# Split products instead of plain fp32 ones in the tail of a decoder layer, and its attention heads' outputs split in place

## The reference

```python
x = x + attn(layernorm(x))          # gated delta rule, 16 heads of 128, then @ Wout (2048 x 512)
x = x + xattn(layernorm(x), ctx)    # energy = (ctx Wq^T + bq)(ctx Wk^T + bk)^T; attention = softmax(energy)
                                    # x_m = layernorm(x) @ attention^T          ("attended")
x = x + ffn(layernorm(x))           # logits = xf Wg^T; gate = argmax of softmax, 8 experts of rank 64
                                    # h = xf A^T (8 x 64 = 512 columns), masked to the chosen expert  ("up")
                                    # y = h Bw^T * 4 * prob of the chosen expert                       ("down")
```

## Time and profile before

| | us |
|---|---|
| median of 3 runs | 2031.08 |
| lowest and highest | 2026.42, 2033.64 |
| profiled execution, span from its first to its last instruction (the only time the page has for it) | 2031.7 |
| its stretch from 1589 us to the end (the tail) | 443 |

### The profile page before, as it was taken

How to read it: one execution, slowest core, us unless ns; L and a number is a source line. 1 busy time by engine, 2 the same in 40 slices (tenths; PEclk the granted TensorE clock), 3 DMA queues, 4 the chain that set the end, 5 groups by cost and what they waited for, 6 DMA issues and landing times.

```text
span 2031.7 us, 45678 instructions
## 1 busy us (share of the span) xinstructions
PE 1915.2 (94%) x16962; PEld 1561.4 (77%) x16962; DVE 1128.8 (56%) x2048; ACT 934.1 (46%) x2987; POOL 743.1 (37%) x1143
## 2 busy tenths in 40 slices
PE   5899999999999999999999998999997799999999
PEld 3688888888888888888888887888886565656574
DVE  5656565665656575656656665657563442534433
ACT  2455554646464555646464645555563321213121
POOL 1255453636363554536363535445452000000000
PEclk9899998999998999989999999989997899999999
DMA  3011111112010111111120101021114513121110
GB/s 101 16 33 32 33 40 25 34 30 42 22 38 22 38 32 33 39 25 37 28 43 22 38 22 38 23 41 34 31 24 144 146 36 93 42 83 52 55 27 21
DMA packets 220196, 87.10 MB, mean 43 GB/s; under 512 B 138320, under 2 KB 204240, under 8 KB 219280
## 3 DMA queue, kind: packets, MB, share of 16 engines
q1 hardware_dynamic: 220048, 84.83, 16.4%
HBM read 57.28 MB, written 27.53 MB: 42 GB/s over the span
## 4 chain that ended last, share of the span: by engine, by line
PE 49%; issue 25%; POOL 10%; DVE 7%; ACT 4%; DMA 3%; SPq 1%; POOLq 1%; DVEq 0%; ACTq 0%
PE bank L558 17%; PE bank L858 4%; PE bank L808 3%; DVE vT L1406 2%; POOL blkT L1774 2%; PE bank L817 2%; PE bank L770 2%; POOL prod L1770 2%; PE bank L759 2%; PE bank L678 2%; ACT vv L1074 2%; PE bank L802 2%; POOL k_tok L1740 2%; PE bank L824 1%; DMA blkT_d<-blkT 1%
## 5 line engine op out<-in xcount | busy, mean ns | idle before, releaser
L558 PE MATMUL bank<-x_hi,w_hi 128*128 128x512 f32 x1024 | 433.5, 423 | 13.4 <-DVE vT L1406 7.1
L558 PE MATMUL bank<-x_hi,w_lo 128*128 128x512 f32 x1024 | 410.3, 401 | 0.0
L558 PE MATMUL bank<-x_lo,w_hi 128*128 128x512 f32 x1024 | 408.7, 399 | 1.1 <-issue 1.1
L558 PEld LDWEIGHTS bank<-x_hi,w_hi 128*128 128x128 f32 x1024 | 197.9, 193 | 56.1 <-issue 13.9
L558 PEld LDWEIGHTS bank<-x_hi,w_lo 128*128 128x128 f32 x1024 | 196.7, 192 | 43.8
L558 PEld LDWEIGHTS bank<-x_lo,w_hi 128*128 128x128 f32 x1024 | 197.7, 193 | 33.2 <-issue 1.6
L1406 DVE SCALAR_TENSOR_TENSOR qT<-bank,cw,qT 128x511 f32<-128x511 f32 (+2 forms) x192 | 142.1, 747 | 51.1 <-ACT qT L1041 46.5
L1830 POOL TENSOR_TENSOR rstd<-ve,mhalf 128x1 f32<-128x1 f32 x32 | 17.4, 544 | 386.8 <-DVE ve L1588 386.8
L1406 DVE SCALAR_TENSOR_TENSOR kT<-bank,cw,kT 128x511 f32<-128x511 f32 (+2 forms) x192 | 143.3, 747 | 9.9 <-ACT kT L1041 4.9
L1206 ACT ACTIVATE o_tmp<-bank 128x128 f32<-128x128 f32 x256 | 67.4, 278 | 175.5 <-PE bank L824 175.5
L1406 DVE SCALAR_TENSOR_TENSOR vT<-bank,cw,vT 128x511 f32<-128x511 f32 (+2 forms) x192 | 143.2, 746 | 6.8 <-ACT vT L1041 2.3
(11 more groups left out here) (221 smaller groups left out, 4446.2 us busy)
## 6 DMA issues: line engine op xcount, KB each, us to landing
w_raw<-in_w_heads SPq DMA_DIRECT2D x64, 256.0 KB, 2.8
o_d<-og SPq DMA_DIRECT2D x64, 256.0 KB, 2.6
o_raw<-o_d SPq DMA_DIRECT2D x16, 1024.0 KB, 6.2
x_in<-in_x SPq DMA_DIRECT2D x16, 256.0 KB, 3.3
blkN_d<-nT SPq DMA_DIRECT2D x64, 64.0 KB, 2.1
t<-blkT_d SPq DMA_DIRECT2D x64, 64.0 KB, 2.4
wo_raw<-in_w_out SPq DMA_DIRECT2D x4, 1024.0 KB, 9.1
x_res<-in_x SPq DMA_DIRECT2D x16, 256.0 KB, 2.7
```

The source lines that it names most:

```text
L558: last = mm(bank[bk][:, :], w[:, kind % 2, d, :], xx[:, d, b * S:(b + 1) * S], start=(n == 0), stop=(n == 3 * ND - 1))
```

## The change

- attended, up and down are each made of three float32r products of high and low parts, accumulated in the same bank: xlT_hi, xlT_lo with attT_hi, attT_lo; xfT_hi, xfT_lo with a_hi, a_lo; hmT_hi, hmT_lo with b_hi, b_lo. The logits stay plain fp32 on xfT. TensorE waits within a product for the low part.
- ScalarE's copies write the high parts (with xfT also the plain one); VectorE gets ln_low, att_low and hm_low, each a subtraction of the high part from the PSUM bank, 16 per batch. A transpose that takes a bank again waits for the low part too.
- a and b are split once, in batch 0: high parts on ScalarE, low parts on VectorE, in place of a_sb and b_sb.
- o_lo lies where o_raw lies, so load_heads waits for the output product two chunks before, not for its split.
- xlT is held for three chunks instead of four and xfT for two, so that ScalarE's copies of later chunks wait for products (xm_mm, h_mm). hm, hmT and y_out are placed elsewhere, the four heads_over semaphores become one.
- On VectorE the next batch's second o_split moves behind layernorm(1,0), and the low parts are put between the other steps; on ScalarE route(0) moves ahead of ln_copy(1,3).

```diff
@@ sync
-                        sp.wait_ge(olo_done, t - 1)
+                        sp.wait_ge(oproj_mm, t - 1)
@@ tiles
+    a_lo = at(place["a_sb"][0], "a_lo", [P, ND, E * R], F32R)
+    o_lo = at(place["o_raw"][0], "o_lo", [P, 2, H, P], F32R)
+    xlT_hi = tl("xlT_hi", [P, 3, ND, P], F32R)
+    xfT_hi = tl("xfT_hi", [P, 2, ND, P], F32R)
@@ tensor, ln_transpose
                     if n >= 2:
                         pe.wait_ge(lnT_done, 8 * b + n - 1)
+                        pe.wait_ge(lnT_low, 8 * b + n - 1)
@@ tensor, attended
-                        last = mm(bank[c % 2][:, :], xlT[:, c, k, :], attT[:, k, :], start=(k == 0), stop=(k == ND - 1))
+                        mm(bank[c % 2][:, :], xlT_hi[:, c % 3, k, :], attT_hi[:, k, :], start=(k == 0), stop=False)
+                    pe.wait_ge(lnT_low, 8 * b + c + 1)
+                    for k in range(ND):
+                        mm(bank[c % 2][:, :], xlT_lo[:, c % 3, k, :], attT_hi[:, k, :], start=False, stop=False)
+                    if c == 0:
+                        pe.wait_ge(attT_low, 4 * b + 4)
+                    for k in range(ND):
+                        last = mm(bank[c % 2][:, :], xlT_hi[:, c % 3, k, :], attT_lo[:, k, :], start=False, stop=(k == ND - 1))
@@ tensor, up
-                        last = mm(bank[c % 2][:, :], xfT[:, c, k, :], a_sb[:, k, :], start=(k == 0), stop=(k == ND - 1))
+                        mm(bank[c % 2][:, :], xfT_hi[:, c % 2, k, :], a_hi[:, k, :], start=(k == 0), stop=False)
+                        mm(bank[c % 2][:, :], xfT_hi[:, c % 2, k, :], a_lo[:, k, :], start=False, stop=False)
+                    pe.wait_ge(lnT_low, 8 * b + 4 + c + 1)
+                    for k in range(ND):
+                        last = mm(bank[c % 2][:, :], xfT_lo[:, c % 2, k, :], a_hi[:, k, :], start=False, stop=(k == ND - 1))
@@ scalar, ln_copy
+                    if stage == 0:
+                        if c == 3:
+                            act.wait_ge(xm_mm, 4 * b + 1)
+                        fn(xlT_hi[:, c % 3, :, :], grid(2 + c % 2), ACT.Copy).then_inc(lnT_done, 1)
+                    else:
+                        act.wait_ge(h_mm, 4 * b + max(c - 1, 0))
+                        fn(xfT[:, c % 2, :, :], grid(2 + c % 2), ACT.Copy)
+                        fn(xfT_hi[:, c % 2, :, :], grid(2 + c % 2), ACT.Copy).then_inc(lnT_done, 1)
@@ vector
+                def ln_low(stage, c):
+                    dve.wait_ge(lnT_done, 8 * b + 4 * stage + c + 1)
...
+                    tt(low, grid(2 + c % 2), high.bitcast(F32), ALU.subtract).then_inc(lnT_low, 1)
@@ vector, order in a batch
                 maximum(3)
+                ln_low(0, 0)
                 o_split(b, 3)
                 residual(0, 1)
                 attention(2)
                 attention(3)
                 layernorm(0, 1)
+                if first:
+                    for i, (low, raw, high) in enumerate(((a_lo, a_sb, a_hi), (b_lo, b_sb, b_hi))):
+                        dve.wait_ge(ab_hi_done, i + 1)
+                        tt(low[:, :, :], raw[:, :, :], high[:, :, :].bitcast(F32), ALU.subtract).then_inc(ab_lo_done, 1)
+                ln_low(0, 1)
+                att_low(0)
+                att_low(1)
                 residual(0, 2)
                 layernorm(0, 2)
                 if more:
                     o_split(b + 1, 0)
                 residual(0, 3)
+                att_low(2)
+                att_low(3)
                 layernorm(0, 3)
+                ln_low(0, 2)
+                ln_low(0, 3)
+                residual(1, 0)
+                layernorm(1, 0)
                 if more:
                     o_split(b + 1, 1)
-                for c in range(NC):
+                for c in (1, 2):
                     residual(1, c)
                     layernorm(1, c)
+                ln_low(1, 0)
+                residual(1, 3)
+                layernorm(1, 3)
+                ln_low(1, 1)
+                ln_low(1, 2)
...
                 route(0)
+                ln_low(1, 3)
                 route(1)
+                hm_low(0)
                 route(2)
+                hm_low(1)
                 result(0)
                 route(3)
+                hm_low(2)
                 result(1)
+                hm_low(3)
```

More of the change, by code:

```diff
@@ L204, in layer @@
     kx = tl("kx", [P, S])
-    attT = tl("attT", [P, NC, S])
+    hm = at(place["qx"][0], "hm", [P, 2, D])
+    attT_hi = tl("attT_hi", [P, NC, S], F32R)
+    attT_lo = tl("attT_lo", [P, NC, S], F32R)
     x_res = tl("x_res", [P, NC, D])
     xl = tl("xl", [P, 2, D])
[L208 to L212, removed]
+    xlT_hi = tl("xlT_hi", [P, 3, ND, P], F32R)
+    xlT_lo = tl("xlT_lo", [P, 3, ND, P], F32R)
+    xfT = tl("xfT", [P, 2, ND, P])
+    xfT_hi = tl("xfT_hi", [P, 2, ND, P], F32R)
+    xfT_lo = tl("xfT_lo", [P, 2, ND, P], F32R)
+    a_hi = tl("a_hi", [P, ND, E * R], F32R)
+    b_hi = tl("b_hi", [P, E * R // P, D], F32R)
     t_small = Plan(consts_end)
@@ L319, in layer @@
     y_store = [sem("y_store0"), sem("y_store1")]
-    heads_over = [sem(f"heads_over_{e}") for e in ("pe", "act", "dve", "pool")]
+    ab_hi_done, ab_lo_done, lnT_low, attT_low, hmT_low = (
+        sem(n) for n in ("ab_hi_done", "ab_lo_done", "lnT_low", "attT_low", "hmT_low"))
+    heads_over = sem("heads_over")
     held = sem("held")
@@ L477, in _ @@
             head(H - 1, False)
[L480 to L481 removed]
+            sp.wait_ge(heads_over, 4)
             for s in og_out:
@@ L938, in down @@
                     for k in range(E * R // P):
-                        last = mm(bank[4 + c % 2][:, :], hmT[:, c % 2, k, :], b_sb[:, k, :],
-                                  start=(k == 0), stop=(k == E * R // P - 1))
+                        mm(bank[4 + c % 2][:, :], hmT_hi[:, c % 2, k, :], b_hi[:, k, :], start=(k == 0), stop=False)
+                        mm(bank[4 + c % 2][:, :], hmT_hi[:, c % 2, k, :], b_lo[:, k, :], start=False, stop=False)
+                    pe.wait_ge(hmT_low, 4 * b + c + 1)
+                    for k in range(E * R // P):
+                        last = mm(bank[4 + c % 2][:, :], hmT_lo[:, c % 2, k, :], b_hi[:, k, :],
+                                  start=False, stop=(k == E * R // P - 1))
                     last.then_inc(y_mm, 1)
@@ L1241, in _, with batch @@
             o_split(0, 1)
-            def batch(b, more):
+            def batch(b, first, more):
                 def exponentials(m):
@@ L1271, in batch @@
                 o_split(b, 3)
+                if first:
+                    fn(a_hi[:, :, :], a_sb[:, :, :], ACT.Copy).then_inc(ab_hi_done, 1)
+                    fn(b_hi[:, :, :], b_sb[:, :, :], ACT.Copy).then_inc(ab_hi_done, 1)
                 ln_copy(0, 1)
@@ L1555, in o_split, with batch @@
                 tt(o_lo[:, c % 2, :, :], o_raw[:, c % 2, :, :], o_hi[:, c % 2, :, :].bitcast(F32), ALU.subtract).then_inc(olo_done, 1)
-            for s in heads_over:
-                dve.wait_ge(s, 1)
+            dve.wait_ge(heads_over, 4)
             o_split(0, 0)
             o_split(0, 1)
-            def batch(b, more):
+            def batch(b, first, more):
                 def maximum(m):
```

82 lines of the change are left out of this document (54 added, 28 removed).

## The result

The changed kernel takes 2021.12 us (median of 4 runs, 2017.27 to 2023.73) against 2032.36 us before (4 runs, 2026.42 to 2036.67): a ratio of 0.9945, 95% interval 0.992 to 0.997, so faster, by half a percent. The forecast was 2016.9 us, a ratio of 0.993. Counted from these medians the change took 11.2 us; the forecast had 14.2. Its profiled execution took 2023.73 us with a span of 2022.0, so 1.7 us lie around the span, which the page of before did not show.

A forecast was written before the change was run, and what follows sets the result against it. TensorE was taken to bound the tail, working 419.57 of 443 us. Batch gains of 0.55, 4.75, 4.75 and 4.1 summed to 14.2 us, from the 2031.08 median to 2016.9 us; range 2007 to 2030.

The forecast's parts named there:

- rival 1: Clock falls in other batches too, behind 2.9 us idle before up(0): three times 2.0 us, 2022.9 us; chance 0.22.
- (a): The 48 attended, up and down products: 2.73 us each in place of 3.43, 8.5 us per batch, 34 in all.
- (b): Waits for low parts within products, 13 a batch: taken as 0, upper bound 6 us.
- (c): VectorE's 16 low parts per batch: 0.68 us each, 11 us per batch, the cost depending on place.
- (d): o_raw loads waiting for the output product: new stall of 3.4 us in batch 0, 1.2 us in the others.
- (e): Next batch's o_split behind layernorm(1,0): attended(2) runs through, attended(3) waits 1.6 us, net gain 0.5.
- (f): Second layernorm's chunk 2 transpose waits for ln_low: TensorE stands 2.9 us where it stood 0.7, 2.2 more.
- (g): Two xfT buffers instead of four: about 0.75 us of new stall before the expert transpose, 0.1 more behind it.
- (h): Clock: half speed behind batch 0's 3.4 us stall costs 2.0 us; nothing counted for the 2.9 us stalls.
- Rival 2: VectorE chain from residual(1,0) to route(1) longer, 0.2 us more per handover: 2030 us, no measurable change; chance 0.14.
- Rival 3: o_raw loads landing in 9.9 us, the largest seen: 29.5 us lost, so slower at 2046 us; chance 0.06.
- Rival 5: Fewer stalls than walked, half of the 20 us of new stalls and clock absent: 2007 us; chance 0.12.

The follow-up runs named there:

- e3_reorder_only: Kernel before, with only residual(1,0) and layernorm(1,0) moved ahead of the next batch's second o_split on VectorE: tail 432.2 us, ratio to before 0.9955.
- e8_all: Changed kernel with later o_lo, up(0) before ln_transpose(1,2), xfT low parts on GpSimd, second o_lo at batch end, layernorm(0,0) earlier: tail 398.7 us, ratio to before 0.9804.
- e4_inplace_only: Kernel before, with only o_lo placed over o_raw and the loads waiting for oproj_mm: tail 449.0 us, ratio to before 1.0046.
- e5_order: Changed kernel with VectorE's o_lo of chunks 2 and 3 moved behind layernorm(0,0) and layernorm(0,1): tail 428.0 us, ratio to before 0.9941.
- e2_nolow: Changed kernel without VectorE's sixteen low parts per batch and the waits for them, high parts used instead: tail 420.9 us, ratio to before 0.9883.
- e9_all_vector: As e8_all, but with the low parts of xfT on VectorE and none on GpSimd: tail 402.2 us, ratio to before 0.9783.
- e6_up0_first: Changed kernel with TensorE's up(0) ahead of ln_transpose(1,2) and ln_transpose(1,3) behind up(1): tail 420.0 us, ratio to before 0.9919.
- e1_fill: Changed kernel with ten useless matmuls between the second layernorm's chunk 1 and chunk 2 transposes: tail 425.5 us, ratio to before 0.9915.

## Why the prediction was right, and where not

The direction and the range held; 2016.9 us was 4.2 us too low. The sum of the parts did not hold: the tail, where all of its terms lie, gained 7.9 us and not 14.2. That the whole time came out closer is luck: nothing was changed outside the tail, where times scatter. The forecast case, 2012 to 2020, misses 2021.12, and rival 1's 2022.9 is nearer to it. Step by step:

- (a) *Products*: right. 2.72 us for one, against 3.43. The cleanest check is two kernels without the waits: middle steps of e3_reorder_only (104.7 to 105.0) and e8_all (96.3) differ by 8.5 us, the forecast's 8.5 per batch. The estimate from four passes against three, 0.86 us a product or 10.3 us a batch, would have been too high.
- (b) *Waits within a product*: right at 0. Behind a wait or a transpose a product lasts 2.86 us with two such waits in it (attended(0) of batch 1) and 2.85 with one (attended(1)).
- (c) *Price of the low parts*: 0.69 us against 0.68. Right.
- (d) *Loads behind the product*: right in kind, 2.96 us in batch 0 and 1.15, 0.89 and 0.67 for 1.2 in the others, shown alone by e4_inplace_only (9.1 us) and undone by e5_order.
- (e) *The moved o_split*: as walked, with 1.3 instead of 1.6 us before attended(3). e3_reorder_only shows that this part by itself is worth 7.7 us, which the sum hid: in the changed kernel the late load and the low parts use most of it up, and I booked only 0.5 a batch.
- (f), (g) *Waits for ln_low and hm*: 2.73 and 0.45 us for 2.9 and 0.75. e2_nolow shows VectorE's chain as their cause: without the low parts the second is gone and the first is 2.0 us.
- (h) *Clock*: **the step that failed.** "I don't count the clock for the 2.9 us stalls" left out 7.8 us in three batches, and a granted clock near 0.5 behind those stalls was among its own signs of being wrong. The fall that it did count, in batch 0, cost 1.4 us for 2.0 (first to second transposes 14.48 us against 13.05 before). Rival 1 had the mechanism and 6.0 us for the rest, at a chance of 0.22. Its argument against (a short transpose splits the gap, and 2 us gaps now do no harm) did not hold here: transposes did not keep the clock up. Waits of 1.97 us left it up three times in the kernel before, but in e2_nolow and e5_order waits of 2.0 and 2.1 us brought it down in some batches. The warning of idle gaps in the Trainium skill, "TensorE: Matmul & The Clock Gate", section "Why this matters for your kernels", held here where I had given it one chance in five. It is for somewhat longer gaps than these; here 2.73 us was enough in all three batches that had it.

The sum with what was measured: 14.2 - 7.8 = 6.4 us. The forecast's waits (3.4 + 3 x 1.2 + 3 x 1.6 + 3 x 2.9 + 2.35 + 4 x 0.85) add up to 26.2 us, those in the rows to 5.7 + 4.0 + 10.3 + 1.8 = 21.8, so 4.4 more are won, and 0.6 by the cheaper fall in batch 0: 11.4. The tail gave 7.9. The 3.5 between come to some 0.2 us for each of the 15 waits. A wait costs a little more than its idle time in the rows, which the sum of rows leaves out: in e9_all_vector a wait of 0.68 us makes the step 0.9 longer than e8_all's, and before attended(2) a row of 1.97 stands for 2.15 from start to start. Part of the difference may be the scatter of single executions; that was not tested by itself.

Rival 2 (a longer VectorE chain) did not happen: no wait was longer than walked. Rival 3 fell with landings of 6.2 us at most (its terms add up to 28.9 us, not 29.5, which changes its 2046 by nothing that shows), rival 4 with the 2.72 us. Rival 5 is out too: the waits were 4.4 us shorter in all, not half.

## What to carry to other kernels

Price a new wait twice: its length, and what it does to the clock behind it, here up to 3.1 us for 2.7 us of waiting, and 3.2 us for 2.1 in e5_order, on an engine that is otherwise never idle. Before shortening TensorE's work, lay out by hand which engine ends last at each handover; here the shorter products uncovered VectorE's order, and five moves of existing steps were worth about 30 us of tail, the change itself 7.9. Where the work in front of a buffer's reader is put in place to save space, the load's late start matters only for what stands behind it in an engine's stream, so move the urgent steps ahead of it.

## What the hardware showed that I had not expected

- The same wait at the same place does not always cost the same: 2.73 us of idle time was followed by stretches of 5.70, 7.21 and 7.26 us, 2.11 and 2.12 us by 7.30 and 4.13, 2.0 us by 4.16 and 7.33. Waits of 1.06 and 1.09 us were followed by a fall of the clock in e6_up0_first, one of 1.10 us was not. What decides between them is not shown.
- Four 128x128 transposes between two waits did not hold the clock up (0.79 in the window of the changed kernel's batch 1), ten 128x512 matmuls did (1.00 in the same window of e1_fill).
- A VectorE pass from SBUF to SBUF took 1.51 us in place of 0.55 when it began 0.07 us after a GpSimd subtraction that reads SBUF. When it began 0.2 us ahead of one (e8_all), it took 0.55 and the subtraction 1.48 in place of 1.29. Which of the two starts first decides who pays.
